# The random-feature mix of a transformer-like layer: one exact fp32 product replaced by four fp32r products of split operands, and moved behind the first hidden product

## The reference, cut to what matters

```python
x = attn_x                                   # 8 x 1024 rows of 256, fp32
xn = layernorm(x)
# random-feature part
def rfs(xw, ab, AB, gs):
    dot = einsum('...d,rd->...r', xw, ab[:, None] * gs)
    corr = 0.5 * sum(xw * xw, -1)[..., None] * (ab * ab)
    return 1 / sqrt(256) * AB * exp(dot - corr)
s = einsum('bsr,or->bso', rfs(xn, ...), rfs(input_weights, ...))   # 256 features, 256 outputs
# gated network with ternary weights (-1, 0, 1) and a scale per output
h = silu(xn @ w1.T * s1) * (xn @ w2.T * s2)  # 256 -> 1024
h = gelu(h @ h1.T * t1)                      # 1024 -> 1024
h = gelu(h @ h2.T * t2)                      # 1024 -> 1024
out = x + s * silu(h @ w3.T * s3)            # 1024 -> 256
```

## Time and profile before

| | |
|---|---|
| median of 3 runs | 1345.51 us |
| the profiled execution, whole | 1345.51 us |
| its span in the profile | 1343.7 us |
| TensorE busy | 1320.0 us, 98% |
| TensorE weight load busy | 1119.5 us, 83% |
| VectorE busy | 946.5 us, 70% |
| ScalarE busy | 766.2 us, 57% |
| GpSimd busy | 589.1 us, 44% |
| HBM traffic | 150 GB/s over the span |

### The profile page before, as it was taken

How to read it: one execution, slowest core, us unless ns; L and a number is a source line. 1 busy time by engine, 2 the same in 40 slices (tenths; PEclk the granted TensorE clock), 3 DMA queues, 4 the chain that set the end, 5 groups by cost and what they waited for, 6 DMA issues and landing times.

```text
span 1343.7 us, 16732 instructions
## 1 busy us (share of the span) xinstructions
PE 1320.0 (98%) x6428; PEld 1119.5 (83%) x6428; DVE 946.5 (70%) x1205; ACT 766.2 (57%) x1036; POOL 589.1 (44%) x596
## 2 busy tenths in 40 slices
PE   7989999999999999999999999999999999999997
PEld 6867898888988889888888888888898888988887
DVE  7767867778677786678865776656767567665665
ACT  5546655566555664466654666546565565655564
POOL 4556988999899998888880000000000000000000
PEclk9999999999999999999999999999999999999999
DMA  9798432545324552254521444224432244313351
GB/s 360 290 358 304 147 103 96 170 152 174 103 96 149 176 162 90 94 177 156 178 98 63 134 149 141 79 73 147 154 113 79 94 152 133 109 63 120 132 165 40
DMA packets 88372, 193.85 MB, mean 144 GB/s; under 512 B 10464, under 2 KB 12768, under 8 KB 87136
## 3 DMA queue, kind: packets, MB, share of 16 engines
q1 hardware_dynamic: 79520, 160.22, 35.9%
q0 software_dynamic: 8768, 32.51, 6.7%
HBM read 167.53 MB, written 34.60 MB: 150 GB/s over the span
## 4 chain that ended last, share of the span: by engine, by line
PE 92%; DMA 4%; POOL 2%; DVE 1%; issue 0%; ACT 0%; SPq 0%; POOLq 0%
PE ps L211 70%; PE ps L214 21%; DMA ring<-hs 2%; POOL ry L500 1%; DMA ry<-in_h 1%; PE ps L298 1%; DMA s<-in_h 1%; DMA quad<-in_w 1%; POOL quad L500 1%; DMA hs<-ry 0%; POOL s L500 0%; SPq L86 0%; DVE ry L194 0%; DVE split L194 0%; POOL hs L86 0%
## 5 line engine op out<-in xcount | busy, mean ns | idle before, releaser
L211 PE MATMUL ps<-split,ring 128*128 128x512 f32 x2800 | 766.2, 390 | 7.0 <-DMA ring<-hs 5.9
L211 PEld LDWEIGHTS ps<-split,ring 128*128 128x128 f32 x2800 | 526.4, 188 | 118.5 <-DMA ring<-hs 7.6
L194 DVE TENSOR_TENSOR split<-quad,split 128x1024 fp32r<-128x1024 f32 x258 | 338.1, 1319 | 197.4 <-ACT split L190 196.8
L190 ACT ACTIVATE split<-quad 128x1024 fp32r<-128x1024 f32 x258 | 267.1, 1052 | 74.2 <-PE ps L214 74.2
L214 PE MATMUL ps<-split,ring 128*128 128x512 f32 x784 | 305.2, 389 | 0.0
L211 PE MATMUL ps<-xT,w 128*128 128x512 f32 x768 | 216.4, 390 | 0.0
L544 POOL TENSOR_TENSOR cube<-cube,seen 128x256 f32<-128x256 f32 x176 | 194.5, 1105 | 13.8
L190 ACT ACTIVATE quad<-ps 128x512 f32<-128x512 f32 x192 | 114.7, 597 | 140.4 <-PE ps L214 140.4
L190 ACT ACTIVATE quad<-quad,cols 128x512 f32<-128x512 f32 (+1 forms) x194 | 139.0, 718 | 83.0 <-DVE quad L194 81.5
L194 DVE TENSOR_TENSOR quad<-quad 128x1024 f32<-128x1024 f32 x128 | 172.8, 1390 | 0.0
L214 PEld LDWEIGHTS ps<-split,ring 128*128 128x128 f32 x784 | 147.3, 188 | 30.5
(11 more groups left out here) (94 smaller groups left out, 1055.2 us busy)
## 6 DMA issues: line engine op xcount, KB each, us to landing
ring<-hs SPq DMA_DIRECT2D x448, 256.0 KB, 3.5
xin<-in_x SPq DMA_DIRECT2D x17, 512.0 KB, 5.7
s_h<-s SPq DMA_DIRECT2D x16, 512.0 KB, 2.6
seen<-in_h POOLq DMA_DIRECT2D x64, 128.0 KB, 3.6
ry<-in_x SPq DMA_DIRECT2D x15, 512.0 KB, 5.5
out<-ry SPq DMA_DIRECT2D x15, 512.0 KB, 2.6
hs<-in_h SPq DMA_DIRECT2D x4, 1024.0 KB, 19.7
ry<-in_h POOLq DMA_DIRECT2D x8, 512.0 KB, 9.5
```

The source lines that it names most:

```text
L190: return act.mark(lambda e: e.activation(dst, src, func, scale=scale))
L194: return dve.mark(lambda e: e.tensor_tensor(dst, a, b, op))
L211: pe.run(lambda e: e.matmul(dst, stat, mov, start=start, stop=stop, skip_group_check=loose))
```

## The change

The feature is written back to the staging buffer by Exp and then split into F, the third split buffer, hi by ScalarE and lo by VectorE. WS gets a second half and is split too. `mix` takes all four products hi x hi, hi x lo, lo x hi, lo x lo in fp32r: 64 matmuls of 256 columns a tile in place of 16 plain fp32 ones. It is emitted inside the first hidden layer, in front of group (1, 0), thus between products w = 0 and w = 1. The tasks around it move: the sums t1 and t2 into product w = 0 and both splits of t2 in front of the mix. In tile 0 the buffers of v and t1 change places.

```diff
-            WS = sf("WS", [P, KD, D])
+            WS = sf("WS", [P, 2, KD, D], F32R)
 def dots(h, banks):
-                feat[h] = cast(quad[place][:, KD * j + r, :], stage[i][:, :], ex, *quad_free[place], func=ACT.Exp)
+                e = cast(stage[i][:, :], stage[i][:, :], ex, func=ACT.Exp)
+                f = F[:, KD * j + r, :, :]
+                hi = cast(f[:, 0, :], stage[i][:, :], e, *f_free)
+                feat[h] = vv(f[:, 1, :], stage[i][:, :], f[:, 0, :].bitcast(F32), ALU.subtract, hi)
                 stage_free[i] = [feat[h]]
 def mix(h, banks):
-                            [(quad[place][:, KD * j + r, b * P:(b + 1) * P], WS[:, r, :]) for r in range(KD)])
+                            [(F[:, KD * j + r, g, b * P:(b + 1) * P], WS[:, w, r, :]) for r in range(KD) for g in range(2) for w in range(2)])
...
-            mix_done[h] = tok
+            f_free[:] = [tok]
 def features_win():
-                f = vs(WS[:, r, :], WF[:, r, :], amp[:, 2, r:r + 1], None, ALU.mult, None, e, made_w["b2"])
-                ws_done[0] = f
+                f = vs(WF[:, r, :], WF[:, r, :], amp[:, 2, r:r + 1], None, ALU.mult, None, e, made_w["b2"])
+                hi = vcopy(WS[:, 0, r, :], WF[:, r, :], f)
+                ws_done[0] = vv(WS[:, 1, r, :], WF[:, r, :], WS[:, 0, r, :].bitcast(F32), ALU.subtract, hi)
-            at = dict(b11=2, b21=3, b12=4, b22=5, v=1, t1=0, t2=6) if t == 0 else next_at
+            at = dict(b11=2, b21=3, b12=4, b22=5, v=0, t1=1, t2=6) if t == 0 else next_at
-            sums = [sub(L0, n, g) for n in ("t1", "t2") for g in range(2)]
-            if t:
-                for task in sums:
-                    task()
-            mix(h0, (4, 5), L0.at["v"])
-            mix(h1, (6, 7), L0.at["v"])
-            quad_free[L0.at["v"]] = [mix_done[h0], mix_done[h1]]
+            def mixes():
+                mix(h0, (4, 5))
+                mix(h1, (6, 7))
             product_layer(L0, L1, {
-                (0, 0): [] if t else sums[:2], (0, 1): [] if t else sums[2:], (0, 2): [sub(L0, "t3", 0)], (0, 3): [sub(L0, "t3", 1)],
-                (1, 0): [split(L0, "t2", 0)], (1, 1): [split(L0, "t2", 1)], (1, 2): [sub(L0, "t4", 0)], (1, 3): [sub(L0, "t4", 1)],
+                (0, 0): [sub(L0, "t1", 0), sub(L0, "t1", 1)], (0, 1): [sub(L0, "t2", 0)], (0, 2): [sub(L0, "t2", 1)], (0, 3): [sub(L0, "t3", 0)],
+                (1, 0): [split(L0, "t2", 0), split(L0, "t2", 1), mixes, sub(L0, "t3", 1)], (1, 1): [sub(L0, "t4", 0)], (1, 2): [sub(L0, "t4", 1)],
```

More of the change, by code:

```diff
@@ L337, in gated_step, with dots @@
             return done
-        def dots(h, banks, place):
+        def dots(h, banks):
             j = h % 2
@@ L354, in dots, with mix @@
             xT_free[h] = [tok]
-        f_free, feat, mixed, mix_done = [], {}, {}, {}
+        f_free, feat, mixed = [], {}, {}
         s_free = [[], []]
         yt_free, res_free = [], []
-        def mix(h, banks, place):
+        def mix(h, banks):
             j = h % 2
@@ L880, in build @@
             L0.made["b12"], L0.made["b22"] = gated(t, h1, (L0.at["b12"], L0.at["b22"]), side)
-            dots(h0, (4, 5), L0.at["v"])
+            dots(h0, (4, 5))
             if t == 0:
                 features_win()
-            dots(h1, (6, 7), L0.at["v"])
+            dots(h1, (6, 7))
             if t == 0:
```

## The result

The changed kernel takes 1355.52 us (median of 4 executions, 1355.09 to 1355.87), the kernel before 1345.57 (4, 1345.40 to 1345.73). The ratio is 1.0062, interval 1.0045 to 1.0081: slower by 10 us. The prediction had the direction and, in its steady part, the size; it said 1349.5 and its range ended at 1352.6. The time lies outside.

What follows compares the result with a forecast made beforehand. TensorE, busy for 98% of the span, was taken to bound the kernel. Seven packed tiles at +5.2 us and the first tile at -1.2 us gave +4.0 us on 1345.5, so 1349.5 us, range 1346.2 to 1352.6.

Steps and rivals of the forecast that it cites:

- The mix on TensorE: Mix in every tile: 64 matmuls at 0.120 us, 7.66 us instead of 6.92; +0.74 us a tile, +5.2 us in seven packed tiles.
- The step from 256 back to 512 columns costs nothing visible: TensorE behind the mix: groups around the `down` products keep their pace, so returning to 512-column matmuls adds no visible time.
- The return from plain fp32 to fp32r has a price: First group behind the old mix: 2.02 us against 1.81, so 0.21 us a tile that the change takes away.
- Rival 1: The mix's new matmuls run at 0.108 us, 6.9 us in all as before; about 1343.5 us, faster; chance 0.05.
- Bank 4 in the packed tiles: Between mix and product w = 1: bank free at 243.4 us, wanted at 244.9; 1.5 us of slack, so no cost.
- Rival 4: Bank 4 is late in each tile, ScalarE's copies standing behind the splits of t2; 1356 us; chance 0.08.
- The first tile: Tile 1: the mix's 0.74 us is hidden by a ring fetch landing earlier; -1.2 us, bounds -4 and +3.
- The stop near 81: TensorE's stop at 81.10 us in tile 1, which should go as the last sum piece for w = 2 is stored earlier.
- GpSimd was to take 7 us: GpSimd's four additions in tile 1: about 7 us instead of 8.84, with VectorE less full beside them.
- for the landing I take 1.2 us earlier: Ring fetch for w = 4 in tile 1, before at 102.01 us: lands 1.2 us earlier, bounds 4 earlier and 3 later.
- rival 3: The first tile gives nothing, or a bank 4 stop comes on top, with stores in the crowded time; 1351.7 us; chance 0.15.
- The sum: Whole kernel: +5.2 - 1.2 = +4.0 us on the profiled execution's 1345.5 us, so 1349.5 us.

Runs made afterwards that it cites:

- three_terms: The changed kernel with the product lo x lo left out of the mix (48 matmuls a tile, not 64): 1346.13 us, ratio 0.9994 to the kernel before.
- lower group: The faster of two clusters of executions of the unaltered changed kernel: six of 14 took 1350.9 to 1351.9 us, the other eight 1354.8 to 1356.6 us.
- again_rounds: The changed kernel unaltered, run again for many executions on one chip: 1354.88 us (median of 10), ratio 1.0059 to the kernel before.
- guarded pair: The changed kernel and the kernel before, each with GpSimd's first additions held back until VectorE has normalised the second half: 1352.54 us and 1345.34 us.
- again_p2: The changed kernel unaltered, one more profiled execution, which fell among the slower ones: 1355.23 us.
- again_p1: The changed kernel unaltered, one more profiled execution, which fell among the faster ones: 1351.85 us.

## Why the prediction was wrong, by its own steps

**The mix on TensorE: right.** 64 x 0.120 = 7.66 us was forecast, 7.67 measured; 164.36 a tile, 164.42 measured. "The step from 256 back to 512 columns costs nothing visible" was not quite so: 0.07 us a tile. "The return from plain fp32 to fp32r has a price" was a misreading without harm to the sum: the 0.21 us are the end of the last plain fp32 matmul. Rival 1 (0.108 us) is out. The Trainium skill gives four passes for plain fp32 ("FP8 and Floating Point Precision", TensorE Precision Notes) and 2.5 ns beyond the columns for a warm matmul ("TensorE: Matmul & The Clock Gate", Wait - 56ns, not 53.3ns?). An estimate from these made the exchange free; the trace of after decides against it for fp32r of 256 columns, with 0.120 us.

**Bank 4 in the packed tiles: right in the sum, wrong in the slack.** No stop came before w = 1 in tile 2. But of the 1.5 us of slack, 0.1 was left. VectorE and ScalarE in the second tile after:

```profile
226.96 1.19 DVE L194 TENSOR_TENSOR F<-rows,F 128x512 fp32r<-128x512 f32 x1 [1.36 <-ACT F L190]
...
235.98 1.07 DVE L194 TENSOR_TENSOR F<-rows,F 128x512 fp32r<-128x512 f32 x1 [1.36 <-ACT F L190]
236.98 8.01 DVE L194 TENSOR_TENSOR quad<-quad 128x1024 f32<-128x1024 f32 x5
```

```profile
243.34 1.06 ACT L190 ACTIVATE split<-quad 128x1024 fp32r<-128x1024 f32 x1 [0.27 <-DVE quad L194]
244.30 2.04 ACT L190 ACTIVATE s<-ps 128x512 f32<-128x512 f32 x4
```

The first copy ends near 244.9, and w = 1 begins at 245.01. I had priced the low parts at 0.68 us, their price alone; three of four took 1.07 to 1.19 beside GpSimd's count, and the sums began at 236.98, not 235.5. `three_terms`, which wants the bank 1.9 us earlier, shows that the slack was gone: 6.8 us of waiting in its first four tiles. Rival 4 was nearer than its 0.08.

**The first tile: the wrong step of the lower group.** Forecast -1.2 us, measured +0.75. Its parts: w = 1 to end at 79.0 and w = 2 at 86.2; they ended at 78.5 and 85.7. Bank 4 was to cost 0.5; 0.36. The stop near 81 was to go; it went. GpSimd was to take 7 us; 6.08. What failed is "for the landing I take 1.2 us earlier". Counted from the tile's start TensorE goes on behind it 55.22 - 53.00 = 2.2 us later, inside the bound of 3, and the three pieces in front of it were late as well, which I had not priced. Behind the landing 1.5 us came back, 1.16 of them the stop for ScalarE at 123.94 that this execution does not have; that gives +0.75. It is the outcome of rival 3, which I had weighed at 0.15. Its mechanism, the stores of `s` in the crowded time, is not shown, and neither is my other idea, that raw copies that start earlier meet more of the ring fetches (`again_rounds` has them 1.5 us later than the first profile and a tile as long, 174.57): why the pieces land later stays open. The guarded pair shows +3.5 for the first tile, so its size differs from run to run. In the profiled pair this is 1.95 us of error; the start, 0.64 shorter, and the steady part, 5.8 instead of 5.2, nearly cancel. Against this execution of the lower group the forecast is 1.9 us low.

**The sum: the step that failed the prediction.** "The profiled execution took 1345.5 us whole, the same as the median, so 1349.5 us." I took one execution's start as the kernel's, and put what the start can add at nothing without a reason. The start holds a race between data for GpSimd and three VectorE instructions of 0.15 us. Which comes first decides over 3.4 us in the two profiles (start +6.1, first tile -2.7) and over some 4 us between the groups, and the median of the changed kernel fell on the other side. Against the lower group the same forecast lies inside the range, so with 13 of 33 executions in that group it was partly chance on which side the median fell. The change does not touch that code, and why the changed kernel falls on this side more often stays open. The rows to see it stood in the trace of before, VectorE and GpSimd at the start:

```profile
23.12 0.16 DVE L204 SCALAR_TENSOR_TENSOR sm<-sm 128x4 f32<-128x4 f32 x1
...
23.40 5.41 POOL L500 TENSOR_TENSOR s<-s 128x512 f32<-128x512 f32 x4 [6.58 <-DMA s<-in_h]
```

0.12 us lie between the end of the one and the start of the other. I read no row of the start.

## What to carry to other kernels

A profile is one execution. Before adding a term to it, look for places where two engines' first use of a shared port depends on when a DMA lands, and give the range both outcomes. A price that was read alone (0.68 us) is not the price in the stretch where the other engine works, and a slack worked out from such prices is smaller than it looks. A fetch that is issued while the DMA engines are full was not sooner there for being issued sooner: 1.8 us earlier at the issue, 1.6 us later at the landing.

## What the runs showed of the hardware

- An fp32r matmul of 256 columns has the pace 0.120 us in `down` and in the mix (64 in a row: 7.67 us), 0.013 us beyond its columns at 2.4 GHz, the same excess as one of 512 columns (0.227 us). A plain fp32 one of 256 columns takes 0.431 us from start to start, and the row of the matmul behind it starts some 0.2 us before it is done.
- A VectorE instruction of 128x4 elements took 0.15 us alone and 0.81 to 1.30 us when it met GpSimd's first additions; a cast to fp32r of 128x256 took 0.29 and 1.27 to 1.33 us.
- TensorE's granted clock averaged 0.57 and 0.58 over the 8 us behind stops of 1.42 and 2.67 us in the start of `again_p2`; in `again_p1`, with stops of 0.61 and 1.30 us there, it stayed at 1.00. In the first tile it was 0.50 behind a stop of 2.85 us. What such a stop costs is more than its own length: the tile of `again_p2` begins 6.1 us later than that of `again_p1`, with 3.5 us more of stops for L204.
